# Adding the value bias as two bf16 parts, with the first three row-tile loads behind the weights

## The reference, cut to what matters

```
x = layernorm(x + attn(x));  x = layernorm(x + moe(x))
attn:  q1,q2 = [x, x_prev] @ W1_q, W2_q;  k1,k2 = x @ W1_k, W2_k     # 16 heads of 4
       L_q, L_k = exterior(q1,q2), exterior(k1,k2), normalised        # 6 numbers a head
       p = softmax(causal(L_q (J L_k)^T / sqrt(6)))
       v = x @ W_v + b_v
       out = (p v) @ W_o + b_o
moe:   8 experts, top 2 of a softmax router, silu(x Wg) * (x Wu) @ Wd
```

## Time and profile before

| | |
|---|---|
| median of 3 runs | 4478.61 us (4477.79 to 4530.11) |
| the profiled execution, its time | 4477.94 us |
| its span, slowest core (core 5) | 4476.4 us |
| spans of the 8 cores | 4463.3 to 4476.4 us |
| PE busy | 3357.0 us (75% of the span) |
| DVE busy | 1148.3 us (26%) |
| ACT busy | 980.0 us (22%) |
| mean granted clock of PE, core by core | 0.763 to 0.764 |

### The profile page before, as it was taken

The page is one execution under the profiler, slowest core; times in us unless marked ns, Lnnn a source line. Parts: engine busy times, 40 slices in busy tenths (PEclk is TensorE's granted clock), DMA queues, the critical chain, the costliest instruction groups (busy, mean ns, idle before and its releaser), DMA issues. The chain is left out here.

```text
span 4476.4 us, 49636 instructions; the slowest of 8 cores (4463.3 to 4476.4 us)
## 1 busy us (share of the span) xinstructions
PE 3357.0 (75%) x14564; PEld 1310.0 (29%) x14564; DVE 1148.3 (26%) x3416; ACT 980.0 (22%) x1972; POOL 95.1 (2%) x42
## 2 busy tenths in 40 slices
PE   3555432556867886788855979899898979899897
PEld 1222222111112112111112434344343434344342
DVE  2333354233222113211132111121212112121216
ACT  0000000323534563466620101011010101011010
POOL 0000000000000000000000000000000000000000
PEclk8666655555555555555556999999999999999999
DMA  4111122000000000000007051514215051512401
GB/s 74 34 33 34 38 76 60 14 12 10 1 12 10 1 1 12 10 1 1 1 15 78 1 52 26 52 26 46 33 10 69 1 52 27 52 26 27 52 1 76
DMA packets 214908, 129.34 MB, mean 29 GB/s; under 512 B 188656, under 2 KB 188656, under 8 KB 214656
## 3 DMA queue, kind: packets, MB, share of 16 engines
q0 software_dynamic: 200832, 75.83, 14.7%
q1 hardware_dynamic: 13824, 50.34, 3.6%
HBM read 191.99 MB, written 8.39 MB: 45 GB/s over the span
## 5 line engine op out<-in xcount | busy, mean ns | idle before, releaser
L803 PE MATMUL pD<-wd_sb,ht 128*128 128x512 bf16 x2816 | 628.2, 379 | 197.0 <-DVEq L821 188.5
L483 ACT ACTIVATE PT<-pS 128x512 bf16<-128x512 f32 (+3 forms) x1280 | 612.9, 530 | 365.4 <-PE pS L473 353.5
L504 PE MATMUL pAV<-PT,Vs 128*65 128x512 bf16 (+3 forms) x1280 | 623.8, 563 | 87.5 <-DVEq L493 42.8
L784 PE MATMUL pU<-xfT,wu_sb 128*128 128x512 bf16 x2816 | 666.9, 380 | 25.5 <-DMA wu_sb<-w_up 25.5
L774 PE MATMUL pG<-xfT,wg_sb 128*128 128x512 bf16 x2816 | 667.8, 380 | 1.0 <-DVEq L753 1.0
L790 ACT ACTIVATE sG<-pG 128x512 bf16<-128x512 f32 x352 | 210.2, 597 | 1751.2 <-PE pG L774 1751.2
L793 DVE TENSOR_TENSOR ht<-sG,pU 128x512 bf16<-128x512 bf16 x352 | 241.8, 687 | 1000.6 <-PE pU L784 1000.6
L803 PEld LDWEIGHTS pD<-wd_sb,ht 128*128 128x128 bf16 x2816 | 266.2, 97 | 559.1 <-issue 256.5
L784 PEld LDWEIGHTS pU<-xfT,wu_sb 128*128 128x128 bf16 x2816 | 275.8, 98 | 359.3 <-issue 28.1
L774 PEld LDWEIGHTS pG<-xfT,wg_sb 128*128 128x128 bf16 x2816 | 276.1, 98 | 335.1 <-issue 4.5
L473 PE MATMUL pS<-LQT,JLKT 6*128 6x512 bf16 (+3 forms) x1280 | 357.9, 537 | 4.3 <-ACT PT L483 2.0
(11 more groups left out here) (121 smaller groups left out, 1323.8 us busy)
## 6 DMA issues: line engine op xcount, KB each, us to landing
wg_sb<-w_gate POOLq DMA_DIRECT2D x8, 2816.0 KB, 26.0
wu_sb<-w_up POOLq DMA_DIRECT2D x8, 2816.0 KB, 24.9
wd_sb<-w_down POOLq DMA_DIRECT2D x8, 2816.0 KB, 19.7
xa<-x_kv SPq DMA_DIRECT2D x32, 512.0 KB, 3.6
xa<-xq SPq DMA_DIRECT2D x16, 512.0 KB, 3.6
xa<-xq_prev SPq DMA_DIRECT2D x16, 512.0 KB, 3.6
xqr<-xq SPq DMA_DIRECT2D x16, 512.0 KB, 3.6
out_q<-outst SPq DMA_DIRECT2D x16, 512.0 KB, 2.6
```

Of the source, the lines that this page charges most:

```text
L483: P.emit("scalar", lambda s, sb=sb, off=off, pslot=pslot, ncols=ncols: s.activation(PT[pslot][:, 0:ncols], pS[sb][:, off:512], AF.Exp, bia ...
L504: return te.matmul(pAV[hb][:, off:512], Vs[:, kc, h, :], PT[pslot][:, 0:ncols], start=(kc == 0), stop=(kc == K - 1))
L784: ins = te.matmul(pU[gi][:], wu_sb[:, hc * 8 + dc, :], xfT[:, dc, tc * 512:(tc + 1) * 512], start=(dc == 0), stop=(dc == 7))
L803: ins = te.matmul(pD[:, nb * 512:(nb + 1) * 512], ht_sb[:, hc, t * 128:(t + 1) * 128], wd_sb[:, hc, nb * 512:(nb + 1) * 512], start=(hc == ...
```

## The change

Four edits, all in block A.

1. The row b_v is loaded as float32, into row 0 of the buffer `xa0`, instead of being converted by the DMA into `bvrow`. DVE then makes two bf16 rows of it: `bvrow`, the cast, and `bvrow_lo`, the rest. These two operations (with a drain between them) take the place of the memset of `zrow`, and stand before the drain that raises `z0` to 2.
2. `zrow` is gone.
3. The loads of row tiles 0, 1 and 2 wait for `z0` at 2, since `xa0` holds the bias until then. The code puts the wait on all three.
4. In each of the 32 PE bursts, the three last matmuls (512, 512 and 128 columns) become four of 512 columns: high and low part for each half. The last group's matmul of 128 columns closes its own accumulation.

```diff
-                zrow = sbA("zrow", [1, 128], BF16)
+                bvrow_lo = sbA("bvrow_lo", [1, D], BF16)
...
-                P.emit("gpsimd", lambda g: g.dma_start(out=bvrow[0:1, :], in_=bvb_h[0:1, :]), inc="wA", inc_n=16)
+                P.emit("gpsimd", lambda g: g.dma_start(out=xa0[0:1, :], in_=bvb_h[0:1, :]), inc="wA", inc_n=16)
...
                 P.emit("vector", lambda v: v.memset(ones1a[:], 1.0), waits=[("wA", W_SETUP)])
-                P.emit("vector", lambda v: v.memset(zrow[:], 0.0))
+                P.emit("vector", lambda v: v.tensor_copy(bvrow[0:1, :], xa0[0:1, :]))
+                P.emit("vector", lambda v: v.drain())
+                P.emit("vector", lambda v: v.tensor_tensor(bvrow_lo[0:1, :], xa0[0:1, :], bvrow[0:1, :], ALU.subtract))
                 P.emit("vector", lambda v: v.drain(), inc="z0")
...
+                    dwaits = [("cast", idx - 2)]
+                    if idx < 3:
+                        dwaits.append(("z0", P.val("z0")))
                     P.emit("sync", lambda sy, s=src_ap, r=row0, bb=b: sy.dma_start(
                         out=xa[bb][:], in_=s[r:r + 128, :]),
-                        waits=[("cast", idx - 2)], inc=xs, inc_n=16)
+                        waits=dwaits, inc=xs, inc_n=16)
...
                                 ins = te.matmul(pV[b][:, n0:n1], xT[tb][:, dc, :], wvks[:, dc, n0:n1],
-                                                start=(dc == 0), stop=False)
-                        te.matmul(pV[b][:, 0:512], ones1a[:], bvrow[0:1, 0:512], start=False, stop=True)
-                        te.matmul(pV[b][:, 512:1024], ones1a[:], bvrow[0:1, 512:1024], start=False, stop=True)
-                        ins = te.matmul(pV[b][:, 1024:1152], ones1a[:, 0:128],
-                                        zrow[0:1, 0:128], start=False, stop=True)
+                                                start=(dc == 0), stop=(dc == 7 and n0 == 1024))
+                        te.matmul(pV[b][:, 0:512], ones1a[:], bvrow[0:1, 0:512], start=False, stop=False)
+                        te.matmul(pV[b][:, 0:512], ones1a[:], bvrow_lo[0:1, 0:512], start=False, stop=True)
+                        te.matmul(pV[b][:, 512:1024], ones1a[:], bvrow[0:1, 512:1024], start=False, stop=False)
+                        ins = te.matmul(pV[b][:, 512:1024], ones1a[:], bvrow_lo[0:1, 512:1024], start=False, stop=True)
```

## The result

The changed kernel took 4503.96 us at the median of 42 runs (from 4500.72), the kernel before 4479.5 (from 4477.12) in as many. The ratio is 1.0065, with a 95% interval of 1.0045 to 1.0085: some 20 to 38 us slower, which is well under 2% and clear of no change. The forecast was 4500, range 4488 to 4511.

The account below looks back on a forecast made before the run. A chain of DVE and PE taking turns, not busy time, was taken to bound the loop. Burst's end 12.5, clock 5.8 and start 3.2 make 21.5 us on 4477.94, 4499.4; with 0.7 for the median, 4500, range 4488 to 4511.

Parts of the forecast that it names:

- The chain: Key-tile loop: DVE and PE take turns, DVE waits for the burst's last matmul, so added burst length is paid 32 times.
- The burst's end: Closing matmuls of each PE burst: four instead of three end 0.39 us later an iteration, 12.5 us in all.
- the bound of 0.43: Burst's end: upper bound an iteration, 13.8 us in all, if two matmuls on one PSUM half cost a little more.
- Tight packing: Rival at the burst's end: the two added one-row matmuls overlap with their neighbours; chance 0.03.
- The clock's answer: Loop's bursts: more fall on the long side, so 0.57 us an iteration instead of 0.39, 5.8 us more; bounds -26.6 and +19.5.
- The walk through the 32 iterations: Loop followed with clock rises kept in the rows' rhythm: it grows by about 0.57 us an iteration, not 0.39.
- the slope and the jump: Later bursts shorten by half the slip, from about 6.6 to 5.2 us for 24 matmuls, then jump back to the longest.
- the loop locks on the long bursts: Rival in the loop: all bursts long, 12.5 + 3.2 + 19.5 = 35 us slower, 4514; chance 0.08.
- The start: Before the loop: tile 0 cast 5.5 us later after the weights, weights 2.3 us sooner; +3.2 us, bounds -0.4 and +5.5.
- The rest, 0: Attention and experts after the loop: these blocks shift but do not change, 0 us.
- a difference beyond 600 us: Sign in the later blocks: if the time there differs, a coupling to them was missed.

Follow-up runs that it names:

- the closing matmuls alone: Kernel before with only the four closing matmuls of 512 columns in place of three, start unchanged: loop 504.4 us, +20.2; whole ratio 1.005 (1.0032 to 1.0068).
- the start alone: Changed kernel with the three closing matmuls of before, loads of tiles 0 to 2 still waiting: loop 483.8 us, whole ratio 1.0009 (0.9995 to 1.0023).

## Why the prediction was right

**The chain.** Right. Every iteration grew, and DVE's first operation still waited for the last closing matmul. The strongest sign is the kernel with the key columns first: releasing DVE before the v matmuls took 183 us out of the loop with the same work.

**The burst's end, 0.39 us.** Right, by a hair too large: 1.03 - 0.66 = 0.37 from the timeline, starts 0.22 us apart, as by columns alone (gate matmuls of 512 columns in the experts, at a granted clock of 1.00, start 0.216 us apart, and 896 columns at that rate are 0.38). Two matmuls behind each other on one half of PSUM start 0.22 to 0.23 us apart, on different halves 0.21, so the bound of 0.43 is not reached. Tight packing is refuted by the same starts.

**The clock's answer, 5.8 us.** I called it the least certain term. What it rests on can be read in the trace of the kernel before. The three bursts of the earlier trace rows on core 5, each cut where the granted clock rises:

```profile
87.28:89.61 2.33, 2.33 (x12) 0.95 (x9) 0.42 (x1) 0.00 (x0) 0.00 (x0) 0.50 0.03 7
89.61:92.41 2.80, 2.80 (x18) 1.35 (x17) 0.00 (x0) 0.00 (x0) 0.00 (x0) 1.00 0.00 0
102.20:106.67 4.47, 4.47 (x18) 1.86 (x15) 0.42 (x1) 0.00 (x0) 0.00 (x0) 0.50 0.00 0
106.67:108.38 1.71, 1.71 (x11) 0.76 (x10) 0.00 (x0) 0.00 (x0) 0.00 (x0) 1.00 0.00 0
118.49:123.74 5.25, 5.25 (x21) 2.21 (x18) 0.42 (x1) 0.00 (x0) 0.00 (x0) 0.50 0.00 0
123.74:125.06 1.32, 1.32 (x9) 0.58 (x8) 0.00 (x0) 0.00 (x0) 0.00 (x0) 1.00 0.00 0
```

| burst starts | clock rises | time at 0.50 | 24 matmuls, to L314 |
|---|---|---|---|
| 87.28 | 89.61 | 2.33 | 5.13 |
| 102.20 | 106.67 | 4.47 | 6.18 |
| 118.49 | 123.74 | 5.25 | 6.57 |

Between the first and the second 2.14 us more at 0.50 make the burst 1.05 longer, between the second and the third 0.78 more make it 0.39 longer: half of the slip, as the prediction has it. The trace's records have only two values of the granted clock, 0.50 and 1.00, on all 8 cores. In the third burst a matmul that follows one of 512 columns starts 0.427 us after it at 0.50, against 0.216 at 1.00 in the experts; those are 1.20 and 2.37 columns a ns, and that is what 1.2 and 2.4 GHz stand for in what was written before the result and the runs. The three rises are 17.06 and 17.07 us apart, and over the loop of all 8 cores every distance between two rises is a multiple of 3.41 us: this is the rhythm. In the 248 bursts of the 8 cores from the second on, the rise came 2.17 to 5.59 us after the burst's start and the 24 matmuls took 5.06 to 6.74 us. Those two ends are 3.42 us apart, one step of the rhythm; I read that as the jump back to the longest. In the changed kernel, on cores 0 to 3, they are 1.83 and 5.54 us, so the place of the jump is not sharp.

The measured term is 18.3 us in 31 iterations less 31 x 0.37 = 11.5, so 6.8; with the closing matmuls alone it is 20.2 - 11.5 = 8.7. The walk through the 32 iterations that gave 0.57 us an iteration is not shown in the prediction; the loop grew by 0.59 (0.65 with the closing matmuls alone). The forecasts before the experiments, made with the result in hand, were 17 to 19 for 20.2, 32 to 35 for 38.2, 36 to 38 for 38.4 and -14 for -15.1. So the slope and the jump carry, and their weak side is the size near the step. That the term stayed small owes something to luck in the size of the edit: with one more matmul of 0.22 us it is 38.2 - 31 x 0.59 = 19.9 us. I had that as a rival with nothing in the rows for it ("the loop locks on the long bursts", 4514). The lock exists, one matmul away, and my bound for it, 19.5 us, was about its size: with six closing matmuls the three rises from 218.58 us on (core 0; 235.65, 252.71) are again 17.07 and 17.06 us apart, with one burst to each.

**The start, 3.2 us.** Measured 2.3. The weights came 3.1 us earlier (2.3 forecast) and tile 0 was cast 5.3 us later after them (5.5 forecast), so the one gain was taken too small and the delay a little too large. Of the signs that I had named, SP's first loads came at 29.98 us on core 0 (31), W_v landed after 17.7 (18 to 19) and the first cast was at 34.07 (35.6), all three early because the weights came sooner than I had taken. Tile 1 wasn't hidden on core 0, by 0.57 us; on cores 1 to 3 it was.

**The rest, 0.** This step was wrong by a few us. I had written that a difference beyond 600 us would mean a coupling that I missed, and there is one: attention is longer by 2.1 us in the mean of 8 cores, with the edit at the start and not with the closing matmuls alone. On cores 0 to 3 the table has +0.5, +1.4 and +1.4, and only the last, the experts, is within the scatter from core to core. The sum 18.3 + 2.3 is 20.6, forecast 21.5; the means of cores 0 to 3 moved by 23.9 and the medians by 24.5. The loop came as forecast (12.5 + 5.8 = 18.3); what the forecast of 4500 lacks is this term.

## What to carry to other kernels

Ask at a burst's end who waits for its last matmul: what is added there is paid at every turn of the loop, and reordering the burst so that the waiting engine's columns come first was worth 183 us here, over seven times what the change cost. Where the profile shows bursts that begin at a granted clock of 0.50 and end at 1.00, as here, don't price an edit by its length alone; measure one step beyond it as well, since 0.22 us cost 19.9 us at one place and 0.2 at the next. Of loads that are put behind the weights count both sides: here tile 0 was cast 5.3 us later after the weights, and the weights were in 3.1 us earlier.

## What the runs showed of the hardware

- In the loop of the kernel before, the granted clock was 0.50 at the start of each burst from the second on and 1.00 at its end, and its rises lay a multiple of 3.41 us apart. With 2.14 us more of it at 0.50 a burst was 1.05 us longer.
- The granted clock and the loop lock to each other. With +0.59 us and +0.81 us at the burst's end the loop took the same 522 us; three neighbouring bursts with +0.81 us were 17.05 and 17.15 us apart and the rises 17.07 and 17.06, five steps of 3.41 us. The bursts looked at ran at a granted clock of 0.59 to 0.61 where three neighbours of the kernel before had 0.77, 0.65 and 0.62. With five closing matmuls the clock rose 5.42 us into a burst of 6.64, with six 5.04 us into one of 6.47.
- With row-tile loads of SP beside it the weights' queue was slower: W_v took 20.5 us to land with three tiles beside it, 18.9 with two and 17.7 with none.
- The same attention instructions take one of two times, about 3 us apart, and the edit at the program's start shifts which of them most cores get (7 of 8 cores short before, 7 of 8 long after, 7 of 8 long with the start alone). How is open.
